# Attention of the first stage: one mask product for a chain of four heads, three probability buffers, value products four steps behind

## The chip, the core and the metric

The kernel runs on one core of a Trainium2 chip. The metric is the device time of one execution in microseconds (us); a version's time is the median of its runs. Engines are named as in the profile: PE (TensorE, matrix products; PEld its weight loads), DVE (VectorE), ACT (ScalarE), POOL (GpSimd) and SP (SyncE, which only issues DMAs here).

## What is computed

Two layers, each a cross-attention and a feed-forward part, all with residuals. The change is in the first cross-attention: 8 batches of 256 queries and 256 keys, 32 query heads of width 16 that share 8 groups of keys and values.

```
x = x + jnp.tanh(g_xattn[0]) * _L0_xattn_ref(_layernorm(x, axis=-1), ctx_2048, mask_SxS2_bc0, mask_BxS2_bk0, ...)
...
H, G = 32, 8; HD = 16; HPG = 4
q = X @ Wq.T + bq;  k = enc @ Wk.T + bk;  v = enc @ Wv.T + bv
scores = jnp.einsum('bgrqd,bgkd->bgrqk', q, k) / jnp.sqrt(HD)
scores = jnp.where(causal_mask, -jnp.inf, scores);  scores = jnp.where(padding_mask, -jnp.inf, scores)
w = jax.nn.softmax(scores, axis=-1)
out = jnp.einsum('bgrqk,bgkd->bgrqd', w, v) ... @ Wo.T + bo
```

## The kernel before

Everything is written as f16 high and low halves, so a product is three products (`three`, L140 to L142). The first attention is `phase_a`. Each engine has its own program (`on_sp`, `on_pe`, `on_act`, `on_pool`, `on_dve`), and semaphores order them; no scheduler moves anything. After a prologue each engine runs 8 bodies, one for each batch b, of NS = 32 steps n. Here T(n) means the moment at which PE begins step n of a body.

What a step does, in the order in which each engine is programmed:

- PE: the transposed scores of batch b (`turned_scores`, L748 and L750), keys on the partitions, for two query heads and one half kc of the keys, into one of two PSUM banks; then the products with the values of the step LAG = 3 back (`times_v`, L767, L769, L771, twelve small ones); then plain scores of batch b+1 (`scores`, L727 and L730), which serve only to find each query's maximum. On top of this, at fixed steps: output projection of batch b-1 (`turn_output`, then `output`, one slice of three 512-column products per step, OTURN and OUT), query projections of batch b+2 (PQ), key and value projections (PK), key transposes (L713), the transposes of the maxima (`turn_maxima`, L738, at NEG0 and NEG1).
- ACT: two exponentials of the bank, one to f16 (`ph`, L1031) and one to f32 (`prob`, L1032); at fixed steps the copies `high_q` (L934), `high_kv` (L945 to L951), `take_maxima` (L957), `high_output` (L961), `normal` (L970), and sums or signs of feed-forward weights for the next stage (`absolute`, L987, in bodies 0 to 3 at SUM_AT; `sign`, L996, in bodies 4 to 7 at CUT_AT and LAST_AT).
- POOL: `pl` = `prob` - `ph` (L1143), and at the steps of FRONT the halves of the next context and x tiles.
- DVE: the maxima (`maxima`, L1232), `low_q` (L1206), `low_kv` (L1214 to L1218), `normalise` (L1248, L1251) and others.
- SP: loads of weight pieces (L543) and contexts, DMA transposes of contexts and x (`place_ctx`, `place_x`), of the queries (`place_q`, L559), of the signed weights (`place_piece`, L577), and the copies of the negated maxima into the queries (`place_maxima`, L549). SP works through its list in program order; each entry waits for its own data.

The mask is added by a product of its own: `ident16` times `madd`, 512 columns. A chain is a row of products that add up in one bank. The first product of a chain adds the mask and the scores of one head; the next subtracts these scores and adds those of the next head (keys are stored as a pair, negated beside plain, and a 128-row query chunk holds two neighbouring heads). Before, a chain has two heads, so every second step of each bank has a mask product.

The waits that matter: exponential n waits for `turned_scores(n)` and for `pl` of step n-2 (two `prob` buffers); `turned_scores(n)` waits for the exponential of n-2; `times_v(n-3)` waits for `pl` of n-3. The query projection uses bank BM, which the turned maxima and the output of half 0 use too.

## Time and profile before

| | |
|---|---|
| time, median of 3 runs | 1663.49 us (1662.81 to 1663.49) |
| the profiled execution's own time | 1660.81 us |
| its span, first to last instruction | 1659.1 us |
| granted TensorE clock over the span | 0.984 of full speed |
| first exponential of the attention to the last | 78.7 to 490.6 us |

The span is cut by stage; the eight bodies are 412 us of it, 51.5 us each. A stretch's row gives each engine's busy time within it. In a row of the timeline the columns are start, duration, engine, line, operation, tiles and shape, count, and in brackets the engine's idle time before it with what ended it.

### The profile page before, as it was taken

What the parts mean: (1) busy time and instruction counts of PE and PEld (TensorE: products, weight loads), DVE (VectorE), ACT (ScalarE), POOL (GpSimd) and SP (SyncE); (2) the same over time, 40 slices, a digit from 0 to 9 for tenths busy, and PEclk for the clock granted to TensorE, in tenths of its full rate; (3) what the DMA queues carried; (4) which work ended last, traced back from release to release, by engine and by line L of the source; (5) the groups of instructions that cost most, each with busy time, mean ns of one, the idle gap of its engine ahead of it and who ended that gap; (6) DMA issues with size and microseconds to landing.
All of it is one profiled execution on the core that took longest, in us unless ns stands there. A gap on an engine that the chain in (4) does not pass through costs nothing. (4 is left out here: it accounts for less than half of the span.)

```text
span 1659.1 us, 29208 instructions
## 1 busy us (share of the span) xinstructions
PE 1576.7 (95%) x10826; PEld 828.4 (50%) x10826; DVE 944.3 (57%) x1947; ACT 710.2 (43%) x1311; POOL 831.6 (50%) x893
## 2 busy tenths in 40 slices
PE   5889999999779999999999989999999999999998
PEld 3456665666434444446565644444444444444443
DVE  5756766778847888735656442468454333322246
ACT  3288888888886666523323221211111111233321
POOL 3488887877884555533534244434342542022244
PEclk9899999999899999999999999999999999999999
DMA  7754645333254665433553427546453745388855
GB/s 189 169 119 100 119 94 110 89 80 75 73 130 95 127 121 102 96 83 77 109 124 80 96 65 159 119 97 158 90 108 92 153 111 115 77 190 195 188 154 189
DMA packets 453955, 195.67 MB, mean 118 GB/s; under 512 B 395500, under 2 KB 418286, under 8 KB 453816
## 3 DMA queue, kind: packets, MB, share of 16 engines
q1 hardware_dynamic: 440216, 171.26, 47.6%
q0 software_dynamic: 5680, 18.62, 4.4%
q10 hardware_dynamic: 7920, 3.93, 1.0%
q8 instruction: 88, 1.44, 0.4%
q14 instruction: 51, 0.42, 0.1%
HBM read 77.17 MB, written 22.81 MB: 60 GB/s over the span
## 5 line engine op out<-in xcount | busy, mean ns | idle before, releaser
L1143 POOL TENSOR_TENSOR a_pl<-a_prob,a_ph 128x512 f16<-128x512 f32 x256 | 296.0, 1170 | 74.6 <-ACT a_prob L1032 74.2
L1232 DVE TENSOR_REDUCE a_mx<-bank 128x2 f32<-128x512 f32 x256 | 173.2, 686 | 87.2 <-PE bank L730 85.7
L140 PE MATMUL bank<-XTh,d_whs 128*128 128x512 f16 x512 | 194.9, 381 | 3.9 <-PEq L89 2.4
L141 PE MATMUL bank<-XTl,d_whs 128*128 128x512 f16 x512 | 194.7, 380 | 0.0
L142 PE MATMUL bank<-XTh,d_wls 128*128 128x512 f16 x512 | 194.6, 380 | 0.0
L1031 ACT ACTIVATE a_ph<-bank 128x512 f16<-128x512 f32 x256 | 153.8, 601 | 59.2 <-PE bank L750 36.2
L2420 POOL CAST d_cut<-d_raw 128x512 f16<-128x512 f32 x90 | 57.1, 635 | 227.4 <-DMA d_raw<-in_L_ffn_sw 145.6
L1032 ACT ACTIVATE a_prob<-bank 128x512 f32<-128x512 f32 x256 | 154.0, 602 | 0.0
L2340 DVE TENSOR_TENSOR d_hid<-d_hid,bank 128x512 f32<-128x512 f32 x64 | 43.9, 686 | 169.2 <-PE bank L142 165.3
L2331 ACT ACTIVATE d_hid<-bank 128x512 f32<-128x512 f32 x64 | 38.2, 597 | 204.9 <-PE bank L142 204.9
L2335 ACT ACTIVATE d_hh<-d_hid 128x512 f16<-128x512 f32 x64 | 40.3, 630 | 194.2 <-DVE d_hid L2340 194.2
L2432 POOL DMA_INDIRECT e_x<-rows,d_who x39 | 37.1, 952 | 145.8 <-DMA e_xTl<-e_x 139.8
L2422 POOL TENSOR_TENSOR d_cut<-d_raw,d_cut 128x512 f16<-128x512 f32 x90 | 106.3, 1181 | 7.2
L767 PE MATMUL bank<-a_v,a_ph 128*128 128x17 f16 x1024 | 103.2, 172 | 5.3 <-POOL a_pl L1143 5.1
L730 PE MATMUL bank<-a_qk 128*128 128x256 f16 x512 | 100.1, 279 | 7.8 <-DVE a_mx L1232 7.6
L750 PE MATMUL bank<-a_qk 128*128 128x512 f16 x256 | 99.6, 389 | 6.8 <-ACT a_prob L1032 6.7
L2350 DVE SCALAR_TENSOR_TENSOR X<-bank,tg,X 128x512 f32<-128x512 f32 x112 | 76.3, 744 | 50.1 <-PE bank L142 50.1
L767 PEld LDWEIGHTS bank<-a_v,a_ph 128*128 128x128 f16 x1024 | 88.4, 97 | 28.7 <-POOL a_pl L1143 7.7
L771 PE MATMUL bank<-a_v,a_pl 128*128 128x17 f16 x1024 | 102.1, 171 | 0.0
L769 PE MATMUL bank<-a_v,a_ph 128*128 128x16 f16 x1024 | 101.9, 170 | 0.0
L1535 PE MATMUL bank<-b_wpj,b_hTh 128*128 128x512 f16 x256 | 97.0, 379 | 1.6 <-DMA b_hTl<-b_hcut 1.6
L140 PE MATMUL bank<-d_whd,d_hh 128*128 128x512 f16 x256 | 97.0, 379 | 1.5 <-DVE d_hl L2344 1.5
(350 smaller groups left out, 3978.1 us busy)
## 6 DMA issues: line engine op xcount, KB each, us to landing
d_raw<-in_L_ffn_w SPq DMA_DIRECT2D x48, 256.0 KB, 3.0
d_raw<-in_L_ffn_sw SPq DMA_DIRECT2D x42, 256.0 KB, 3.0
made<-e_y SPq DMA_DIRECT2D x39, 256.0 KB
a_stage<-in_L_ffn_w_fc SPq DMA_DIRECT2D x32, 256.0 KB, 2.9
a_stage<-in_L_ffn_w_proj SPq DMA_DIRECT2D x32, 256.0 KB, 3.0
a_fbuf<-in_ctx SPq DMA_DIRECT2D x16, 256.0 KB, 3.2
rows<-f_cut SPq DMA_DIRECT2D x16, 256.0 KB, 2.5
out_x<-X SPq DMA_DIRECT2D x16, 256.0 KB, 2.4
```

The costliest lines, as they stand in the source:

```text
L140: nc.tensor.matmul(out_ap, lhi, rhi, start=first, stop=False)
L141: nc.tensor.matmul(out_ap, lhi, rlo, start=False, stop=False)
L142: return nc.tensor.matmul(out_ap, llo, rhi, start=False, stop=last_one)
L730: last = nc.tensor.matmul(bk[:, r * S:(r + 1) * S], qT[:, par, 2 * g + r, tt * P:(tt + 1) * P], kT[:, par, 2 * g + half, :], start=False, ...
L767: nc.tensor.matmul(into[:, c:c + HD0 + 1], ph[:, n % NP, q], vv[:, b % 3, kc, g, 0:HD0 + 1], start=first, stop=False, skip_group_check=True)
L769: nc.tensor.matmul(into[:, c:c + HD0], ph[:, n % NP, q], vv[:, b % 3, kc, g, HD0 + 1:VW], start=False, stop=False, skip_group_check=True)
L771: last = nc.tensor.matmul(into[:, c:c + HD0 + 1], pl[:, n % NP, q], vv[:, b % 3, kc, g, 0:HD0 + 1], start=False, stop=(kc == 1), skip_grou ...
L1031: nc.scalar.activation(ph[:, n % NP, :], bank[BST + n % 2][:, :], ACT.Exp)
L1032: nc.scalar.activation(prob[:, n % 2, :], bank[BST + n % 2][:, :], ACT.Exp).then_inc(ev["E"], 1)
L1143: nc.gpsimd.tensor_tensor(pl[:, n % NP, :], prob[:, n % 2, :], ph[:, n % NP, :], ALU.subtract).then_inc(ev["L"], 1)
L1232: nc.vector.tensor_reduce(mx[:, h, tt, half, 2 * (g % 4):2 * (g % 4) + 2], bank[BS + m % 2][:, :].rearrange("p (r k) -> p r k", r=2), AX_X ...
L2422: nc.gpsimd.tensor_tensor(cut[:, i % RING, 1, :], raw[:, i % RING, :], cut[:, i % RING, 0, :], ALU.subtract).then_inc(p_lo, 1)
```

## The change

Chains run over four heads: the mask product stands only where j, the place in a chain of four, is 0, so at steps 0, 1, 8, 9, 16, 17, 24, 25 (before: at 0, 1, 4, 5, 8, 9, ...). One turned product of 512 columns becomes two of 256, since the two heads' query chunks are no longer neighbours. The queries need chunks (q0,q1), (q1,q2), (q2,q3) instead of (q0,q1), (q2,q3), so 30 chunks instead of 16: `place_q` issues 16 DMA transposes per batch instead of 8, the first of its two calls in two parts; for the first batches PE turns the additional chunks (`turn_early`) and ACT takes them (`take_early`). `place_maxima` issues three DMAs instead of two. There are three `prob` buffers (NR) and five `ph` and `pl` (NP), and LAG is 4. The x tiles have one buffer instead of two. NEG0 goes from step 27 to 20, so the maxima are turned between the two query projections, in bank BM. SUM_AT, CUT_AT, OTURN, OUT, FRONT and the steps of `normal`, `place_ctx`, `place_x` and `load_ctx` move.

```diff
-    NP = 4
-    prob = sb("a_prob", [P, 2, D])
+    NP, NR = 5, 3
+    prob = sb("a_prob", [P, NR, D])
...
-    on = sb("a_on", [P, 2, 2, D])
+    on = sb("a_on", [P, 2, D])
...
-    LAG = 3
+    LAG = 4
...
-    NEG0, NEG1 = 27, 4
-    OTURN, OUT = (5, 6), (7, 11)
+    NEG0, NEG1 = 20, 4
+    OTURN, OUT = (6, 7), (8, 12)
...
-    SUM_AT = [1, 5, 9, 13, 17, 21, 25, 29]
-    CUT_AT = [1, 6, 11, 17, 23, 28]
-    WO_AT = [12, 14, 16, 18]
+    SUM_AT = [1, 3, 9, 11, 17, 23, 29, 30]
+    CUT_AT = [1, 3, 9, 17, 23, 29]
+    WO_AT = [9, 14]
...
     def which(m):
-        u = m % 16
-        return u // 8, 4 * (m // 16) + 2 * (u // 4 % 2) + u % 2, u // 2 % 2
+        return m % 2, m // 16, m // 2 % 8
+
+    def key_chunk(h, r, j):
+        first = j == 0 or j == 4
+        return 8 * h + 4 * r + 2 * (j // 4) + (0 if first else 1)
+
+    def query_chunk(h, r, j):
+        if j % 2:
+            return 16 * h + j - 1 + r
+        return 16 * h + j + r if j % 4 == 0 else 16 * h + 8 + j - 2 + r
...
-                if b + 2 < B and n == PQ[1] + KC + 1:
-                    place_q(b + 2, 0)
+                for tt in range(2):
+                    if b + 2 < B and n == PQ[tt] + KC + 1 + tt:
+                        place_q(b + 2, 0, [tt])
...
-                if f < B and n == 10:
-                    place_ctx(f)
+                if f < B and n in (8, 12):
+                    place_ctx(f, [n // 12])
...
-                if f < B and n == 22:
-                    place_x(f)
+                if 3 < f + 1 < B and n == NS - 6:
+                    load_ctx(f + 1)
+                if f < B and n == NS - 4:
+                    place_x(f)
...
-            if half == 0:
+            if n % 8 < 2:
                 nc.tensor.matmul(bk[:, :].rearrange("p (r k) -> p r k", r=2), ident16[:, :],
                                  maddT[:, kc, :].unsqueeze(1).broadcast_to([P, 2, S]), start=True, stop=True)
-            nc.tensor.matmul(bk[:, :], kT[:, par, 2 * g + half, kc * P:(kc + 1) * P],
-                             qT[:, par, 2 * g:2 * g + 2, :].rearrange("p r q -> p (r q)"),
-                             start=False, stop=True, skip_group_check=True).then_inc(ev["ST"], 1)
+            for r in range(2):
+                last = nc.tensor.matmul(bk[:, r * S:(r + 1) * S], kT[:, par, key_chunk(h, r, j), kc * P:(kc + 1) * P],
+                                        qT[:, par, query_chunk(h, r, j), :], start=False, stop=True,
+                                        skip_group_check=True)
+            last.then_inc(ev["ST"], 1)
...
-                if b + 3 < B and n == 4:
+                if b + 3 < B and n == 3:
                     moments(b + 3)
```

Three places in the order of the instructions. First PE at step 4 of body 2, from the last product with the values on (`a_madd` is the mask); before:

```order
L771 MATMUL bank<-a_v,a_pl 128x17
L727 MATMUL bank<-a_madd,ident 128x512
L730 MATMUL bank<-a_qk 128x256 x2
L738 MATMUL bank<-ident,a_nmx 16x128 x2
L748 MATMUL bank<-a_maddT,ident 128x512
L750 MATMUL bank<-a_qk 128x512
```

And in the changed kernel:

```order
L817 MATMUL bank<-a_v,a_pl 128x17
L773 MATMUL bank<-a_qk 128x256 x2
L781 MATMUL bank<-ident,a_nmx 16x128 x2
L794 MATMUL bank<-a_qk 128x256 x2
L813 MATMUL bank<-a_v,a_ph 128x17
```

Both mask products of the place are gone, and the turned product is a pair. Second, PE at step 20 of body 2, from its plain scores on; before:

```order
L727 MATMUL bank<-a_madd,ident 128x512
L730 MATMUL bank<-a_qk 128x256 x2
L140 MATMUL bank<-a_wkvh,a_cTh 128x256
L141 MATMUL bank<-a_wkvl,a_cTh 128x256
L142 MATMUL bank<-a_wkvh,a_cTl 128x256
```

And in the changed kernel:

```order
L773 MATMUL bank<-a_qk 128x256 x2
L781 MATMUL bank<-ident,a_nmx 16x128 x2
L140 MATMUL bank<-a_wkvh,a_cTh 128x256
L141 MATMUL bank<-a_wkvl,a_cTh 128x256
L142 MATMUL bank<-a_wkvh,a_cTl 128x256
```

The transposes of the maxima now stand ahead of the last slices of the key projection. Third, SP's list from the end of body 1 into body 2, before:

```order
L559 DMA_TRANSPOSE a_qk<-a_qs 128x4x128 x4
L549 DMA a_qk<-a_nT 1x8x256 x2
L543 DMA a_stage<-in_L_ffn_w_proj 128x512
L516 DMA a_fbuf<-in_ctx 128x512 x2
L559 DMA_TRANSPOSE a_qk<-a_qs 128x4x128 x4
L543 DMA a_stage<-in_L_ffn_w_proj 128x512
L549 DMA a_qk<-a_nT 1x8x256 x2
```

And in the changed kernel, from `place_x` at step 28 of body 1 on:

```order
L559 DMA_TRANSPOSE a_xTh<-a_fcut 128x4x128
L560 DMA_TRANSPOSE a_xTl<-a_fcut 128x4x128
L565 DMA a_stage<-in_L_ffn_w_proj 128x512 x2
L582 DMA_TRANSPOSE a_qk<-a_qs 128x4x128
L586 DMA_TRANSPOSE a_qk<-a_qs 128x3x128
L582 DMA_TRANSPOSE a_qk<-a_qs 128x4x128
L586 DMA_TRANSPOSE a_qk<-a_qs 128x3x128
L582 DMA_TRANSPOSE a_qk<-a_qs 128x4x128
L586 DMA_TRANSPOSE a_qk<-a_qs 128x3x128
L582 DMA_TRANSPOSE a_qk<-a_qs 128x4x128
L586 DMA_TRANSPOSE a_qk<-a_qs 128x3x128
L565 DMA a_stage<-in_L_ffn_w_proj 128x512 x2
```

The query transposes of step 0 are eight instead of four, and the x transposes stand close ahead of them instead of at step 22.

## Rows read from the trace of the kernel before

**Rows 1.** The page: busy time of PE over the span.

```profile
PE 1576.7 (95%) x10826; PEld 828.4 (50%) x10826; DVE 944.3 (57%) x1947; ACT 710.2 (43%) x1311; POOL 831.6 (50%) x893
```

**Rows 2.** Timeline of PE, body 2, steps 1 to 3.

```profile
183.13 0.38 PE L748 MATMUL bank<-a_maddT,ident 128*128 128x512 f16 x1
183.35 0.38 PE L750 MATMUL bank<-a_qk 128*128 128x512 f16 x1
...
185.28 0.38 PE L730 MATMUL bank<-a_qk 128*128 128x256 f16 x2
185.50 0.38 PE L750 MATMUL bank<-a_qk 128*128 128x512 f16 x1
```

**Rows 3.** Stretches: bodies 0, 2, 5, 6, 7; last columns granted clock, DMA share, GB/s.

```profile
78.70:131.00 52.30, 45.90 (x577) 27.42 (x576) 31.26 (x59) 43.07 (x93) 42.89 (x41) 0.98 0.54 114
...
183.00:235.10 52.10, 49.87 (x637) 31.82 (x636) 34.89 (x65) 44.18 (x96) 43.69 (x42) 1.00 0.55 103
...
340.70:391.40 50.70, 49.46 (x636) 31.72 (x634) 36.41 (x65) 42.10 (x84) 37.14 (x32) 1.00 0.29 69
391.40:442.10 50.70, 43.20 (x566) 26.52 (x563) 43.23 (x84) 41.40 (x79) 42.63 (x40) 0.93 0.29 72
442.10:492.20 50.10, 40.25 (x510) 22.11 (x510) 28.54 (x54) 45.78 (x86) 43.98 (x41) 0.92 0.48 110
```

**Rows 4.** Timeline of PE: T(29) of body 1; then body 2's steps 6, 8, 28, 29.

```profile
178.36 0.38 PE L748 MATMUL bank<-a_maddT,ident 128*128 128x512 f16 x1
...
191.49 0.39 PE L730 MATMUL bank<-a_qk 128*128 128x256 f16 x2 [0.81 <-DVE a_mx L1232]
...
193.54 0.38 PE L748 MATMUL bank<-a_maddT,ident 128*128 128x512 f16 x1
...
227.54 0.39 PE L748 MATMUL bank<-a_maddT,ident 128*128 128x512 f16 x1
...
230.01 0.61 PE L713 MATMUL bank<-ident,a_ks 128*128 128x128 f16 x8 [1.13 <-DVE a_v L1218]
...
230.46 0.38 PE L748 MATMUL bank<-a_maddT,ident 128*128 128x512 f16 x1
```

**Rows 5.** Timeline of ACT, body 2, steps 1, 2 and 4.

```profile
184.62 0.59 ACT L1032 ACTIVATE a_prob<-bank 128x512 f32<-128x512 f32 x1
185.09 0.63 ACT L987 ACTIVATE a_tern<-a_stage 128x512 f16<-128x512 f32 x1
...
185.71 0.60 ACT L1031 ACTIVATE a_ph<-bank 128x512 f16<-128x512 f32 x1
...
188.14 0.60 ACT L1031 ACTIVATE a_ph<-bank 128x512 f16<-128x512 f32 x1 [0.38 <-POOL a_pl L1143]
```

**Rows 6.** Timeline of POOL, body 2, steps 3 and 4.

```profile
188.54 2.28 POOL L1143 TENSOR_TENSOR a_pl<-a_prob,a_ph 128x512 f16<-128x512 f32 x2
190.78 1.16 POOL L1080 TENSOR_TENSOR a_fcut<-a_fbuf,a_fcut 128x512 f16<-128x512 f32 x1
```

**Rows 7.** Timeline of all engines, body 2, step 20.

```profile
214.96 0.38 PE L730 MATMUL bank<-a_qk 128*128 128x256 f16 x2
215.07 0.69 DVE L1206 SCALAR_TENSOR_TENSOR a_qs<-bank,a_qs 128x512 f16<-128x512 f32 x1 [0.82 <-ACT a_qs L934]
```

**Rows 8.** SP's issues: body 0; bodies 2 to 3 (first the timeline, then the DMA view).

```profile
79.62 6.24 SPq L559 DMA_TRANSPOSE a_qk<-a_qs  x4
...
225.75 5.12 SPq L559 DMA_TRANSPOSE a_qk<-a_qs  x4
230.91 1.36 SPq L549 DMA_DIRECT2D a_qk<-a_nT  x2
...
a_qk<-a_qs SPq DMA_TRANSPOSE x52, 2.7
```

**Rows 9.** Weight loads in front of the paired products, whole attention.

```profile
L730 PEld LDWEIGHTS bank<-a_qk 128*128 128x128 f16 x512 | 41.5, 98 | 28.7 <-DVE a_mx L1232 10.6 <-issue 3.3
```

**Rows 10.** Stretch: body 0, from POOL's step 0 to its step 15.

```profile
79.83:105.34 25.51, 21.43 (x274) 12.14 (x273) 15.83 (x30) 20.79 (x42) 21.50 (x21) 0.97 0.44 100
```

More of the change, by code:

```diff
@@ L666, in q_of @@
                 pass
+            elif tt and b >= 2:
+                wait("nc", b - 1, 1, 2)
             elif tt:
@@ L716, in scores @@
         def scores(b, par, m):
-            tt, g, half = which(m)
-            bk = bank[BS + m % 2]
+            tt, h, j = which(m)
+            bk = bank[BS + tt]
             wait("M", b, m + 1, NS)
@@ L741, in turned_scores @@
         def turned_scores(b, par, n):
[L742 to L743 removed]
+            kc, h, j = which(n)
+            bk = bank[BST + kc]
             wait("E", b, n + 1, NS)
             if n % 16 == 0:
[L746 to L747 removed]
+                pe.wait_ge(ev[f"ng{h}"], 48 * (b + 1))
+            if n % 8 < 2:
                 nc.tensor.matmul(bk[:, :].rearrange("p (r k) -> p r k", r=2), ident16[:, :],
@@ L754, in times_v @@
+            last.then_inc(ev["ST"], 1)
         def times_v(b, n):
-            g, half, kc = n // 4, n // 2 % 2, n % 2
+            p, j, kc = n // 8, n // 2 % 4, n % 2
             if n % 8 == 0:
-                wait("ON", b, g // 2 + 1, G0 // 2)
-            wait("L", b, n + 3, NS)
-            into = bank[BAV + g // 2 % 2]
+                wait("ON", b, p + 1, G0 // 2)
+            wait("L", b, n + NR + 1, NS)
+            into = bank[BAV + p % 2]
             for r in range(2):
+                g = p + 4 * r
@@ L1017, in on_act @@
         high_kv(0, 1)
+        for i in range(2):
+            for tt in range(2):
+                take_early(0, 1, tt, i)
         for tt in range(2):
@@ L1021, in on_act @@
         take_maxima(0, 0)
+        for i in range(2):
+            for tt in range(2):
+                take_early(1, 0, tt, i)
         normal(2, 0)
```

250 lines of the change are left out of this document (143 added, 107 removed).

## Prediction

> **What bounds the kernel now.** I began with the page. PE is busy for 95% of the span [rows 1], but that is the union of overlapping products and says little here: a 512-column product is shown as 0.38 us, and the next starts 0.22 us after it; a pair of 256 columns takes 0.22 us together [rows 2]. The Trainium skill says the same of that column (Trainium Kernel Development and Optimization, Performance Expectations: matmul busy time is a bad metric because matmuls are pipelined). So I worked in distances between starts.
>
> Next the stretches of the bodies [rows 3]. Bodies 1 to 5 have PE busy for nearly all of their 52 us, with ACT and POOL at 44 and 43.5. Bodies 0, 6 and 7 leave PE idle for 6 to 10 us and are still 50 to 52 us long, so there the engines wait for each other in turn.
>
> Then the timeline of one steady body. From T(29) of body 1 to T(29) of body 2 it is 230.46 - 178.36 = 52.10 us, and falls into three parts [rows 4]: T(29) to T(8), 15.18 us; T(8) to T(28), 34.00 us; T(28) to T(29), 2.92 us. The middle part has a projection slice in every step up to 26, and PE runs without a wait worth naming: products bound it. The third part is a round trip: the key projection's last slice, ACT's copies, DVE's halves, and PE waits 1.13 us to turn the keys [rows 4]. In the first part PE has little to do. There ACT needs 0.47 us per exponential from start to start and 0.62 us for an `absolute` [rows 5], and POOL 1.12 us for a `pl` (188.54 to 190.78 for two) or a low half [rows 6]. With two `prob` buffers ACT may be only two steps ahead of POOL; it waits 0.38 us at step 4 [rows 5]. PE waits 0.81 us for the maxima at step 6 [rows 4], which are late because the moments of step 4 stand ahead of them on DVE.
>
> **The change, part by part,** for a steady body (1 to 3).
>
> Mask products in the middle part. Steps 12, 13, 20 and 21 lose two each: 8 x 0.215 = 1.72 us off a part that products bound. An output slice comes in from step 7 (now 8 to 15): 3 x 0.215 = 0.65. 34.00 - 1.72 + 0.65 = 32.93 us.
>
> The split of the turned product. Two of 256 columns start within the same 0.22 us as one of 512 [rows 2], so it costs nothing while the additional weight load is hidden. The loads of the plain scores, which have this very form, take 98 ns beside the products [rows 9]. The bound above is 256 x 0.098 = 25 us in all if none were hidden; I take 0, since rows 2 show the pairs as they run. The skill has a rule against this (TensorE: Matmul & The Clock Gate, Back-to-back issue gap): in a real stream the spacing is set by both the load and the product, and small products suffer. By that rule part of the 25 us would have to be paid; the trace does not agree for 256 columns, at 0.11 us each.
>
> The third part stays at 2.92: same steps, same copies. Only the 0.36 us copy of the maxima leaves ACT ahead of it; I count nothing.
>
> The first part. The moments stand one step earlier and `normalise` one later, so PE's 0.81 us should go. The third `prob` buffer lets ACT lead POOL by a step more (1.1 us), which covers POOL's additional jobs at steps 4 to 6. ACT then sets T(8): ten pairs of exponentials, 9.5, four `absolute` (29, 30, 1, 3), 2.5, the maxima's copy 0.3, and the 0.6 from T(29) to the first exponential: 12.9 us. That is the lower bound; the upper one is 15.18 as now. I take 13.4, near the lower bound, because the two named waits are what separates them.
>
> Against it, step 20. The maxima are now turned there into bank BM, and this must wait for `low_q` of the first half, which reads that bank. On the trace the plain scores of step 20 end at 214.96 + 0.22, and without the two masks 0.43 earlier, 214.75; `low_q` ends at 215.07 + 0.69 = 215.76 [rows 7]. PE waits 1.0 us, with key and query slices queued behind it, in the part that products bound. The wait is absent before, since the next writer of BM stood in step 21. It could be zero if PE came a step later; I keep 1.0.
>
> Sum: 32.93 + 2.92 + 13.4 + 1.0 = 50.25, 1.85 us less; for three bodies -5.5 us.
>
> SP's list. A transpose takes 1.28 us of SP's time (5.12 for four), 1.56 in body 0, and lands 2.7 us after its issue; two copies of maxima take 1.36 [rows 8]. A body's list grows by 8 transposes and 2 copies, 11.6 us, to about 42 of 50 us. It still fits, but from step 27 on it holds 4 + 4 + 8 transposes and two loads, 21.5 us. They start 4.7 us ahead of T(29) (225.75 against 230.46, rows 8 and 4), so end 16.8 after it. In bodies 1 to 3 what follows is a load needed at step 11, about 0.5 us late, hidden by PE's lead. In bodies 4 and 5 it is `place_piece` of step 1, landed at T(29) + 19.5, for which the `sign` of step 9 waits. ACT would be there at 13.4 + 1.8 + 0.6 + 0.95 = 16.8. So ACT waits 2.7 us; two score banks hide about 1.2 us of that, PE loses 1.5. Body 4: -1.85 + 1.5 = -0.35. Body 5 has no POOL jobs beside `pl` and less to win in the first part (-0.5): -1.72 + 0.65 - 0.5 + 1.0 + 1.5 = +0.9.
>
> Body 0. POOL's first fifteen steps take 25.51 us with 21.50 busy [rows 10]. They are not bound by products, so the third buffer and FRONT's new steps pay: I take 22.0, so -3.5 (bounds 0 and -4.0). The rest of that body: masks off, step 20's wait on, about even.
>
> Bodies 6 and 7. PE is not the bound; POOL is busy 42.6 and 44.0, ACT 41.4 and 45.8 of 50.7 and 50.1 [rows 3]. The buffer smooths, the new CUT_AT avoids the step of `high_output` in DVE and ACT. I take -1.5 and -1.0 (bounds 0 and -4 each).
>
> Prologue. 28 more transposes on PE and eight copies by ACT, a wait for all four query copies; half of the plain scores' masks gone; ACT is mostly idle there. Nothing, within 2 us either way.
>
> Total: -3.5 - 5.5 - 0.35 + 0.9 - 1.5 - 1.0 = -11 us. The later stages are unchanged and take the gain over. The sum is made on the profiled execution, 1660.8 us with 1.7 us outside the span; that is 2.7 below the median, and I carry the difference: 1663.5 - 11 = 1652.5 us.
>
> **The rivals.**
>
> Nearly all mask time comes back (0.14). 128 mask products go, 27.6 us; if step 20's wait and SP's delay stay hidden and ACT sets the first part at its lower bound: 52.1 - 49.0 for bodies 1 to 5, 15 us, with 4 + 3 + 3 elsewhere, 1639. PE's full busy time in bodies 1 to 5 speaks for it; POOL at 43.5 and ACT at 44 of then 49 us speak against it.
>
> The gain is absorbed (0.24). The work only moves to waits: ACT's four `absolute` in the unbound part, the wait at step 20, SP's list. With the first part at 14.8 instead of 13.4 and body 0 at half, -11 + 5 x 1.4 + 1.8: about 1661, from 1656 up.
>
> Slower, by SP's queue (0.08). At body 0's 1.56 us per transpose throughout, 24 transposes are 37.4 us and the rest 10 to 12: the list fills a body, and contexts, weights and x tiles come late in every one. It decides from about 1.5 us per transpose. At 3.5 us lost per body in six bodies, -11 + 21: 1673. The rows of bodies 2 and 3 at 1.28 speak against it.
>
> Slower, by weight loads that aren't hidden (0.02): -11 + 25, 1677.
>
> Slower or even, by the clock (0.03). The granted clock is 0.93 and 0.92 in bodies 6 and 7 [rows 3], where PE has idle time, against 1.00 in bodies 1 to 5. With fewer products PE has more idle time everywhere. Bodies 1 to 5 at 0.92 instead of 1.00 would cost their product-bound parts 8% of 35 us each, 14 us: 1666.
>
> **How the numbers follow.** Forecast 0.49, around 1652.5, from 1645 to 1659 by its bounds. The range 1641 to 1664 leaves out about 0.06 below and 0.13 above. A measurement of this kernel tells no change from 0.2%, 3.3 us. Faster than 1660.2: the forecast, the first rival and a good half of the absorbed case, 0.78. Slower than 1666.8: the queue, the loads, half of the clock, and a tail of the absorbed case, 0.11. Between, 0.11.
>
> **What would show it.** T(8) to T(28) of body 2 near 33.9 us with the wait, and PE's turned maxima at step 20 with about 1.0 us idle, released by DVE's `a_qs`. ACT without waits on POOL in steps 29 to 8. The `sign` of step 9 in bodies 4 and 5 with a wait for a DMA of `a_tern`. SP's sets of four transposes at 5.1 us. Body 0 shortened most. Wrong would be: clock below 1.00 in bodies 1 to 5, body 0 unchanged, or PE starts of the paired products more than 0.11 us apart.

## The result, and the profile after

The changed kernel takes 1670.34 us, median of 7 runs (1667.98 to 1675.61); the kernel before took 1663.49 in the 7 runs beside it. The ratio is 1.0045, with a 95% interval of 1.0028 to 1.0061: 7.5 us slower, where I had forecast 11 us faster. The time lies outside my range.

The stretches of the changed kernel, bodies 0, 2, 5, 6 and 7, answer to [rows 3]; the last row is a piece of body 2:

```profile
75.30:127.00 51.70, 44.08 (x575) 31.23 (x574) 33.64 (x61) 43.12 (x94) 42.48 (x40) 0.87 0.58 127
...
180.80:235.30 54.50, 48.82 (x652) 34.74 (x650) 35.75 (x69) 44.27 (x97) 43.64 (x41) 0.94 0.49 117
...
345.50:404.20 58.70, 50.04 (x655) 34.91 (x653) 37.94 (x68) 41.65 (x85) 37.76 (x33) 0.91 0.42 86
404.20:453.00 48.80, 41.55 (x590) 29.52 (x587) 44.02 (x89) 41.23 (x80) 41.74 (x40) 0.90 0.38 80
453.00:499.40 46.40, 38.43 (x529) 23.99 (x526) 28.33 (x58) 43.65 (x85) 43.15 (x40) 0.89 0.52 121
188.00:194.00 6.00, 4.68 (x43) 3.85 (x44) 3.82 (x8) 5.40 (x13) 4.66 (x6) 0.50 0.45 97
```

Bodies 6 and 7 are 2 us shorter each, as the change wants. Bodies 1 to 5 are longer, body 5 by 8 us, and the granted clock, 1.00 in them before, is 0.91 to 0.97. In the piece of 6 us it is 0.50, which is TensorE at 1.2 GHz. The eight bodies together take 424.1 us, 12.2 more than before; the stretch before them is 3.4 us shorter in this profile and the later stages 1.8 us, which leaves the 7.0 us between the spans of 1659.1 and 1666.1.

Where body 2 is longer shows on PE's timeline, at the places of [rows 4]: T(29) of body 1, steps 5 to 8, step 20, T(28), T(29).

```profile
176.24 0.38 PE L794 MATMUL bank<-a_qk 128*128 128x256 f16 x2
...
187.46 0.39 PE L773 MATMUL bank<-a_qk 128*128 128x256 f16 x2 [1.21 <-DVE a_mx L1298]
189.32 0.61 PE L794 MATMUL bank<-a_qk 128*128 128x256 f16 x2 [1.47 <-ACT a_prob L1099]
...
193.35 0.63 PE L791 MATMUL bank<-a_maddT,ident 128*128 128x512 f16 x1
...
216.01 0.28 PE L781 MATMUL bank<-ident,a_nmx 128*16 128x128 f16 x2 [0.90 <-DVE a_qs L1272]
...
227.89 0.38 PE L794 MATMUL bank<-a_qk 128*128 128x256 f16 x2
...
230.78 0.38 PE L794 MATMUL bank<-a_qk 128*128 128x256 f16 x2
```

T(29) to T(8) is 193.35 - 176.24 = 17.11 us, against 15.18 before and 13.4 forecast. T(8) to T(28) is 34.54, T(28) to T(29) 2.89. In this body the loss sits in the first part. PE waits there first for DVE's maxima, then for ACT; after the second wait its products are half as fast (0.63 instead of 0.38 us in the records). ACT's timeline says what it stood for at its step 3:

```profile
187.57 0.63 ACT L1048 ACTIVATE a_tern<-a_stage 128x512 f16<-128x512 f32 x1 [2.16 <-DMA a_stage<-in_L_ffn_w_proj]
...
365.69 0.72 ACT L1057 ACTIVATE a_tern<-a_stage,a_unround 128x512 f16<-128x512 f32 x1 [6.47 <-DMA b_wfc<-a_tern]
```

The last row is step 9 of body 5, in the middle part of that body. SP's timeline, which answers to [rows 8], has both causes: the load of step 29 (the first of the two at 183.81) stands behind query and x transposes, and in body 5 the piece of step 1 (363.24) stands at the end of a row of transposes that begins at 337.42.

```profile
172.46 1.50 SPq L582 DMA_TRANSPOSE a_qk<-a_qs  x1
...
181.85 1.91 SPq L560 DMA_TRANSPOSE a_xTl<-a_fcut  x1
183.81 1.05 SPq L565 DMA_DIRECT2D a_stage<-in_L_ffn_w_proj  x2
...
337.42 1.20 SPq L582 DMA_TRANSPOSE a_qk<-a_qs  x1
...
351.06 1.19 SPq L582 DMA_TRANSPOSE a_qk<-a_qs  x1
...
360.50 2.70 SPq L586 DMA_TRANSPOSE a_qk<-a_qs  x1
363.24 1.26 SPq L604 DMA_TRANSPOSE b_wfc<-a_tern  x1
```

### The profile page after: what moved, and what is told of

The parts are those of the page before. It is cut to its first block and busy times, and to the rows that moved or that the text cites. A ratio compares the mean times of both kernels' runs of the same rounds, so it can differ in the third digit from the quotient of the medians.

```text
span 1666.1 us, 29689 instructions
## 1 busy us (share of the span) xinstructions
PE 1560.3 (94%) x11014; PEld 849.8 (51%) x11014; DVE 948.8 (57%) x1979; ACT 716.3 (43%) x1319; POOL 832.1 (50%) x893
## 3 DMA queue, kind: packets, MB, share of 16 engines
q1 hardware_dynamic: 463128, 176.74, 47.9%
## 5 line engine op out<-in xcount | busy, mean ns | idle before, releaser
L794 PE MATMUL bank<-a_qk 128*128 128x256 f16 x512 | 106.7, 293 | 23.3 <-ACT a_prob L1099 23.0
L773 PE MATMUL bank<-a_qk 128*128 128x256 f16 x512 | 102.3, 284 | 15.8 <-DVE a_mx L1298 15.6
L142 PE MATMUL bank<-d_whd,d_hl 128*128 128x512 f16 x256 | 97.0, 379 | 0.0
```

Source lines behind the costliest of these rows:

```text
L142: return nc.tensor.matmul(out_ap, llo, rhi, start=False, stop=last_one)
L773: last = nc.tensor.matmul(bk[:, r * S:(r + 1) * S], qT[:, par, query_chunk(h, r, j), tt * P:(tt + 1) * P], kT[:, par, key_chunk(h, r, j), ...
L794: last = nc.tensor.matmul(bk[:, r * S:(r + 1) * S], kT[:, par, key_chunk(h, r, j), kc * P:(kc + 1) * P], qT[:, par, query_chunk(h, r, j), ...
```

## The experiments

Sixteen variants were measured, each beside the kernel before. The table gives their ratios, and the length of each body in the profiled execution, from ACT's first exponential of one body to that of the next (body 7: to the start of its last one). The bodies come from one execution each. The code behind the attention is the same in all of them but for a few semaphores, and the stretch from the last exponential to the end still differs by up to 7.7 us between the profiles (1164.8 to 1172.5), so a difference of a few us between two medians need not come from the bodies.

| kernel | median us | ratio, interval | bodies 0 to 7, us |
|---|---|---|---|
| before | 1663.5 | | 52.4, 52.0, 52.1, 53.2, 52.3, 50.8, 50.7, 48.5 |
| changed | 1670.34 | 1.0045 (1.0028, 1.0061) | 51.7, 53.8, 54.5, 56.1, 54.1, 58.7, 48.8, 46.4 |
| a1_lists | 1660.31 | 0.9971 (0.9955, 0.9986) | 51.1, 51.8, 51.8, 53.5, 53.0, 54.5, 47.9, 46.4 |
| a2_q14 | 1668.51 | 1.0020 (1.0006, 1.0035) | 50.7, 54.3, 54.2, 55.4, 54.2, 56.4, 49.0, 46.3 |
| a3_fill | 1680.54 | 1.0092 (1.0075, 1.0109) | 51.3, 54.6, 54.6, 55.6, 56.1, 59.2, 50.3, 46.8 |
| a4_rings | 1677.36 | 1.0066 (1.0047, 1.0084) | 52.2, 54.5, 55.9, 55.3, 54.1, 57.8, 51.4, 47.9 |
| b1_moments | 1666.85 | 1.0038 (1.0021, 1.0056) | 52.1, 52.9, 53.9, 54.6, 53.5, 57.6, 47.9, 46.3 |
| b2_lists_moments | 1655.48 | 0.9954 (0.9937, 0.9970) | 51.5, 50.2, 52.6, 56.1, 52.1, 51.5, 46.9, 46.2 |
| b3_all | 1655.39 | 0.9947 (0.9931, 0.9964) | 49.0, 54.4, 51.4, 51.7, 53.0, 50.4, 48.0, 46.3 |
| b4_fill | 1669.75 | 1.0035 (1.0021, 1.0048) | 50.3, 53.7, 53.7, 54.7, 54.4, 53.6, 50.6, 47.0 |
| a6_oldsum | 1667.62 | 1.0022 (1.0008, 1.0036) | 49.6, 53.8, 53.0, 53.7, 55.6, 55.7, 50.1, 46.2 |
| c1_front | 1673.45 | 1.0053 (1.0037, 1.0069) | 56.2, 54.6, 53.2, 56.8, 58.7, 51.7, 47.0, 46.4 |
| c2_front_oldsum | 1671.99 | 1.0054 (1.0036, 1.0072) | 56.3, 55.5, 53.6, 55.2, 59.0, 50.2, 49.3, 46.2 |
| c3_front_q14 | 1665.79 | 1.0014 (0.9995, 1.0034) | 54.8, 53.4, 52.3, 55.6, 53.6, 50.3, 48.0, 46.3 |
| e1_lists2 | 1661.17 | 0.9982 (0.9965, 1.0000) | 50.8, 51.8, 51.8, 54.3, 54.4, 52.6, 48.0, 46.4 |
| e2_extras | 1698.97 | 1.0210 (1.0190, 1.0230) | 59.2, 60.8, 60.5, 58.9, 58.4, 52.8, 51.8, 47.7 |
| e3_spread | 1665.77 | 1.0011 (0.9997, 1.0025) | 51.9, 51.6, 51.7, 52.7, 53.0, 51.8, 52.0, 48.5 |
| e4_list | 1707.73 | 1.0245 (1.0217, 1.0272) | 53.3, 58.4, 63.3, 57.6, 67.4, 58.1, 51.6, 48.5 |

### SP's list relieved

```diff
-                if b + 1 < B and n == 0:
+                if b + 1 < B and n == 2:
                     place_q(b + 1, 1)
...
-                if f < B and n == NS - 4:
+                if f < B and n == NS - 2:
                     place_x(f)
```

> The changed kernel, with two entries of SP's list moved and nothing else: the eight query transposes of step 0 stand at step 2, behind the loads and placements of step 1, and the x transposes of step 28 stand at step 30, behind the load of step 29. List theory (my first): the stage loads and the placements are late because SP stands in transposes; ACT waits for them (2.2 to 2.6 us at step 3 of bodies 1 to 3, 7.0 us at step 9 of body 5), PE runs dry behind ACT and the clock falls after it. Then these waits are gone, bodies 1, 2, 3 are about 2 us shorter each, body 5 about 6, and with the clock that is held up the time is 1655 to 1660 us. Step-20 theory (the loss is the wait for the low half at step 20, before the maxima are turned): SP's list is slack, the time stays at 1667 to 1671. Clock theory (fewer products alone let the granted clock fall): the half-clock time in the bodies stays near 68 us and the time within 3 us of the changed kernel's.

Measured: 1660.31 us, 10 below the changed kernel and at the upper edge of what the list theory gave, from two moved places in a list. No `absolute` waits for a load any more, bodies 1 to 3 are 2.0 to 2.7 us shorter, body 5 by 4.2, and bodies 1 and 2 are again at clock 1.00. The list theory holds; the step-20 theory and the clock theory, as sole causes, fall. PE's timeline of body 2 shows what was hidden behind it, two waits for DVE's maxima (1.21 and 0.99 us), and T(8) at 188.31; T(29) of body 1 was at 173.36, so the first part is 14.95 us, and T(8) to T(28) is 222.28 - 188.31 = 33.97.

```profile
173.36 0.38 PE L794 MATMUL bank<-a_qk 128*128 128x256 f16 x2
...
184.58 0.39 PE L773 MATMUL bank<-a_qk 128*128 128x256 f16 x2 [1.21 <-DVE a_mx L1298]
186.47 0.39 PE L773 MATMUL bank<-a_qk 128*128 128x256 f16 x2 [0.99 <-DVE a_mx L1298]
...
188.31 0.38 PE L791 MATMUL bank<-a_maddT,ident 128*128 128x512 f16 x1
...
222.28 0.38 PE L794 MATMUL bank<-a_qk 128*128 128x256 f16 x2
```

DVE's timeline of the same kernel has the reason: moments, their two short operations, a maximum, a copy of keys and the normalisation in one row, busy from 180.68 to 187.6.

```profile
180.68 0.68 DVE L1298 TENSOR_REDUCE a_mx<-bank 128x2 f32<-128x512 f32 x1
181.27 1.28 DVE L1243 BATCH_NORM_STATS2 a_stats<-X 128x6 f32<-128x512 f32 x2
...
182.87 1.06 DVE L1249 TENSOR_SCALAR a_ve<-a_mv 128x2 f32<-128x2 f32 x1
183.84 0.68 DVE L1298 TENSOR_REDUCE a_mx<-bank 128x2 f32<-128x512 f32 x1
184.45 0.68 DVE L1291 COPY a_qk<-bank 128x1024 f16<-128x1024 f16 x1
...
185.73 1.88 DVE L1298 TENSOR_REDUCE a_mx<-bank 128x2 f32<-128x512 f32 x3
```

### The wait at step 20 taken away

```diff
-    PQ, PK = (15, 21), (19, 25)
+    PQ, PK = (14, 21), (19, 25)
```

> The changed kernel, with the first query projection one step earlier (its slices at steps 14 to 17, its halves at 18), so that the low half is done well before the maxima are turned at step 20. Step-20 theory: PE's wait of 1.0 to 1.3 us in six bodies goes, 6 to 8 us off, 1661 to 1664 us. List theory: the wait at step 20 goes as well, but the bodies are longer in their first third, and what PE gains from step 20 on it has partly given to the round trip of steps 28 and 29: 2 to 5 us off. Clock theory: PE has even more slack elsewhere, no change.

Measured: PE's waits before the turned maxima fall from 12.5 us (12 waits) to 3.6 in the whole program, T(8) to T(28) of body 2 is 34.03 instead of 34.54, and the median is 2 us lower (4 us by the ratios, whose intervals overlap a little). The wait exists as I had forecast it, 0.9 us, but of the 0.7 us that go in body 2 the body keeps 0.1, since its first part is longer by as much as the middle part gained. The wait was a term of my sum, so it doesn't explain why the sum failed.

### The removed products put back

```diff
+            if n % 8 in (4, 5):
+                nc.tensor.matmul(bk[0:P // 2, :].rearrange("p (r k) -> p r k", r=2), zero[:, :],
+                                 maddT[:, kc, :].unsqueeze(1).broadcast_to([P, 2, S]), start=False, stop=True,
+                                 skip_group_check=True)
```

and the same for the plain scores.

> The changed kernel, with a product of 512 columns by zeros (added into 64 rows of the same bank) in each place where the kernel before had its second mask, so that PE has the work of before and everything else is of after. Clock theory: the half-clock time in the bodies falls from 68 us towards the 16 us of before, and the time is the same or shorter, 1662 to 1670 us, in spite of 128 more products. List theory: the waits for a_stage and a_tern stay as they are; the part of bodies 1 to 5 that products bound is 1.7 us longer each, and the time is 1675 to 1682 us; the clock recovers only where the idle stretches get shorter than now.

Measured: 1680.54, 10 us above the changed kernel, as the list theory had it. But bodies 1 to 5 together are only 2.9 us longer (280.1 against 277.2), although each has 16 more products, and bodies 1 to 4 ran at clock 1.00. Body 2, then its T(29) of body 1 and T(8), and ACT's wait for the load of step 3:

```profile
182.40:237.10 54.70, 53.36 (x668) 35.23 (x666) 36.32 (x69) 44.34 (x98) 43.73 (x41) 1.00 0.53 115
```

```profile
177.56 0.40 PE L799 MATMUL bank<-a_maddT,a_zero 128*64 128x512 f16 x1
...
192.85 0.38 PE L796 MATMUL bank<-a_maddT,ident 128*128 128x512 f16 x1
...
188.45 0.63 ACT L1057 ACTIVATE a_tern<-a_stage 128x512 f16<-128x512 f32 x1 [1.36 <-DMA a_stage<-in_L_ffn_w_proj]
```

ACT still waits for the load, and yet the first part is 192.85 - 177.56 = 15.29 us, 1.8 less than the 17.11 of the changed kernel and 0.3 more than the 14.95 of a1_lists. So most of what the late load costs in the first part is paid at half clock, and the wait itself is the smaller share: PE's waits there add up to 3.2 us in the changed kernel and 2.7 in a1_lists. (The products put back also fill PE's waits, to 0.3 us in all, so a3_fill alone doesn't part the two.) The same shows in steps 6 to 8, T(6) to T(9), which took 6.42 us at half rate in body 2 of the changed kernel and 4.18 at full rate in body 2 of b2_lists_moments, below. The clock theory holds in part, then: the clock fell where there were fewer products and a late load in one place. Fewer products and 2.7 us of waits, as in bodies 1 and 2 of a1_lists, did not bring it down.

### The buffers of before

```diff
-    NP, NR = 5, 3
+    NP, NR = 4, 2
...
-    LAG = 4
+    LAG = 3
```

> The changed kernel, with the buffers of before: two of prob, four of ph and pl, products three steps behind. If the deeper buffers give what I forecast for them (body 0 3.5 us, the first third of the bodies about 1 us each, bodies 6 and 7 1.0 to 1.5 us), the time is 8 to 12 us longer, 1678 to 1682. List theory: in bodies 1 to 3 ACT stands at the load anyway, so only bodies 0, 6 and 7 lose, 3 to 6 us, 1673 to 1676. If the deeper buffers are themselves the harm (products further behind, all in a bunch at a body's start), it is faster than 1668.

Measured: 1677.36, 7 us longer by the medians and 3.5 by the ratios, whose intervals overlap; the median lies between the ranges of the two theories. Bodies 1 to 5 are together as long as with the deeper buffers (277.6 against 277.2), bodies 0, 6 and 7 lose 0.5, 2.6 and 1.5. That is the pattern of the list theory, and it speaks for the deeper buffers in bodies 6 and 7, though it is one profile against one. POOL's steps 0 to 15 of body 0, on which my term for that body rests, take 22.5 us here with two `prob` buffers and 22.4 in the changed kernel with three (25.5 before): what shortened them was not the third buffer.

### DVE's moments, alone and with the list

```diff
-                if b + 3 < B and n == 3:
+                if b + 3 < B and n == 9:
                     moments(b + 3)
-                if b + 3 < B and n == 8:
+                if b + 3 < B and n == 12:
                     mean(b + 3)
...
-                    if n == 5:
+                    if n == 10:
                         deviation(b + 3)
```

> The changed kernel, with the moments of a body taken by DVE at step 9 instead of step 3 (POOL's power at 10 instead of 5, the mean at 12 instead of 8). DVE theory: the change stacked 2.7 us of moments, a copy of keys and a normalisation in steps 3 and 4, where PE's steps are shortest, so PE waits 1.2 us (2.2 us once SP's list is relieved) for the maxima. In the changed kernel alone ACT stands at the load of step 3 at the same time, so DVE's share is mostly hidden: 1 us or less a body in bodies 0 to 4, 1664 to 1670 us. If DVE was the cause by itself and the loads only waited beside it, the gain is 2 us a body, 1660 to 1662.

Measured: 1666.85. The five waits of `absolute` for loads are still there (8.6 us), and bodies 1 to 3 are 0.6 to 1.5 us shorter: mostly hidden behind the load, as expected.

For the next run the moments stand at step 9 too, SP's list is relieved as in a1_lists, and the eight query transposes are split:

```diff
-                if b + 1 < B and n == 0:
-                    place_q(b + 1, 1)
+                if b + 1 < B and n in (2, 6):
+                    place_q(b + 1, 1, [n // 6])
...
-                if f < B and n == NS - 4:
+                if f < B and n == NS - 2:
```

> The changed kernel with SP's list relieved (x transposes behind the load of step 29, four query transposes at step 2 and four at step 6) and the moments at step 9. Two causes in a row, SP's list and then DVE: with both gone PE's waits for the maxima (2.2 us in bodies 1 to 3, 1.6 in 0 and 4) and for the placed maxima in body 5 (1.8) go, bodies 1 and 2 come near the 50.25 us that I forecast, 8 to 10 us below the run with the lists alone: 1650 to 1653 us. If the moments only push DVE's lateness to step 10, in the part that products bound, the gain is under 3 us, 1657 to 1660.

Measured: 1655.48, 15 us below the changed kernel and 7.7 below the kernel before by the ratio. It is a version that beats both, but it lies between my two ranges. PE's timeline of body 1, T(29), T(8), T(28), T(29):

```profile
124.05 0.38 PE L794 MATMUL bank<-a_qk 128*128 128x256 f16 x2
...
137.22 0.38 PE L791 MATMUL bank<-a_maddT,ident 128*128 128x512 f16 x1
...
171.34 0.38 PE L794 MATMUL bank<-a_qk 128*128 128x256 f16 x2
...
174.22 0.38 PE L794 MATMUL bank<-a_qk 128*128 128x256 f16 x2
```

That is 13.17 + 34.12 + 2.88 = 50.17 us. Two single stalls remain in this profile: POOL stood 6.0 us for a written context in body 2 (my list puts the second half of the query transposes ahead of it, a likely reason that was not tried), and DVE's product of 2 elements took 4.43 us in body 3.

### The early projection on top

> The run with lists and moments mended, and the first query projection one step earlier. With the first third of a body free of waits the wait for the low half at step 20 is on the path: 0.7 us (what the early projection took off the stretch from step 14 to 20) to 1.2 us in six bodies, 4 to 7 us below the run without it, about 1646 us. If the slack is taken by turned outputs and the round trip again, as when it was tried alone (2 us), 1649 to 1651.

Measured: 1655.39, the same as without it. The wait at step 20 of body 1 fell from 0.9 to 0.2 us; in its place stands a wait of 2.4 us for POOL's `pl` there. My expectation of 4 to 7 us was wrong, and so was the smaller one beside it.

### The products put back, without the waits

> The run with lists and moments mended, with the 512-column products by zeros in the places of the removed masks. Mask products in the part that products bound are worth 1.72 us a body as I forecast, and little elsewhere: 1.7 x 6 plus up to 3, so 10 to 13 us longer than the run without them. In the changed kernel itself putting them back cost 10 us with the waits in place, 3.6 of it in bodies 1 to 5. Clock theory: they keep the granted clock up (under 15 us at half rate in the bodies, against some 30 without), and cost only 3 to 6 us.

Measured: 1669.75, 14 us longer, at clock 1.00 in bodies 0 to 5, so just beyond even my larger expectation of 10 to 13. Of the 15.3 us between the two profiled spans 10.4 lie up to the end of the attention, 4.9 in the unchanged stages behind it. In the stretches (body 0 and body 1, without and with the products) the clock shows too: body 0 runs at 0.89 without them and at 1.00 with them, and is no longer for it, in one profile of each.

```profile
77.10:128.60 51.50, 44.36 (x581) 30.67 (x579) 33.11 (x62) 42.96 (x94) 42.45 (x40) 0.89 0.60 123
128.60:178.70 50.10, 46.43 (x651) 33.15 (x649) 36.87 (x69) 43.55 (x97) 43.36 (x41) 1.00 0.54 125
```

```profile
76.70:126.90 50.20, 46.12 (x597) 30.73 (x595) 32.18 (x62) 42.59 (x93) 42.37 (x40) 1.00 0.59 132
126.90:180.70 53.80, 52.96 (x668) 35.25 (x666) 35.19 (x69) 44.31 (x98) 43.74 (x41) 1.00 0.49 115
```

The price of a product by zeros is higher than that of a mask, though. It has 64 columns of weights, and around it PE leaves gaps:

```profile
158.28 0.27 PE L142 MATMUL bank<-a_wkvh,a_cTl 128*128 128x256 f16 x1
158.48 0.40 PE L799 MATMUL bank<-a_maddT,a_zero 128*64 128x512 f16 x1
158.81 0.39 PE L803 MATMUL bank<-a_qk 128*128 128x256 f16 x2
```

The next product starts 0.33 us after it, a mask's 0.215 after; and it starts 0.20 after a product of 256 columns, 0.11 the usual distance. That is 0.42 us each, with eight in the middle part: 3.4 us. Its T(8) to T(28) is 36.45, 2.5 more than the 33.97 of a1_lists, and of the wait at step 20 some 0.9 us are gone in it: 3.4. So the middle part pays for every product in full, and my 8 x 0.215 = 1.72 for the masks in it stands, by this working; masks of the true size were not put back. What they are worth in all was not measured either: the 14 us are an upper bound.

### ACT's extras at the old steps

```diff
-    SUM_AT = [1, 3, 9, 11, 17, 23, 29, 30]
-    CUT_AT = [1, 3, 9, 17, 23, 29]
+    SUM_AT = [1, 5, 9, 13, 17, 21, 25, 29]
+    CUT_AT = [1, 6, 11, 17, 23, 28]
```

> The changed kernel, with ACT's extras at the steps of before (absolute values at 1, 5, ..., 29, signs at 1, 6, 11, 17, 23, 28). The load of step 29 is then wanted at step 9 and the piece placed at step 28 at step 6. If the loads were late because SP's longer list met the changed spread, the wait of 2.2 us at step 3 of bodies 1 to 3 goes with the spread alone, and DVE's wait (2.2 us) stays: 1 us a body, and in bodies 4 and 5 the sign waits elsewhere: 1664 to 1668 us. If SP's list is late for everything it holds, the wait only moves to another step and the time is 1669 to 1672.

Measured: 1667.62. No `absolute` waits for a load, DVE's wait of 2.0 us stays; in body 5 a sign waits 4.8 us for a placed piece. A load that has more steps until its use bears the late list. The time is in the range that I gave for this case, 1664 to 1668.

### The x tile's normalisation later

```diff
-                    if n == 10:
+                    if n == 13:
                         deviation(b + 3)
...
-                if b + 3 < B and n == 12:
+                if b + 3 < B and n == 14:
                     mean(b + 3)
...
-                 17: (x_high, 0), 19: (x_low, 0), 22: (x_high, 1), 24: (x_low, 1)}
+                 19: (x_high, 0), 21: (x_low, 0), 24: (x_high, 1), 26: (x_low, 1)}
```

with ACT's copies at 16 and 18, on top of b2_lists_moments.

> The changed kernel with SP's list and the moments mended as before, and the normalisation of the next x tile one to three steps later (power at 13, mean at 14, ACT's copies at 16 and 18, POOL's halves at 19, 21, 24, 26), so that POOL does not stand for the written context (6.0 us once) and DVE's 2-element product does not stand beside POOL's full row (4.4 us once). If those two stretches were what is left, bodies 2 and 3 come to 50.5 to 51.5 us and the time to 1648 to 1651. If they are single events of one profile, the median stays at 1653 to 1656.

> The run c1_front with ACT's extras at the steps of before. The changed spread puts four absolute values (2.5 us) between steps 29 and 3, where ACT sets the length of a body's first third; the old one puts two there. If ACT sets it, 1.2 us a body come off in bodies 1 to 3 and something in 4 and 5: 4 to 5 us below c1_front. If the round trip of the keys sets the start of that third, nothing.

> The run c1_front with the first query projection one step earlier. The wait at step 20 (1.2 us) goes for 0.5 to 0.7 us a body, as in the two runs that had it; if nothing takes it back, 3 to 4 us below c1_front. In those two runs the medians moved by 2 and 0 us; if that is the rule, less than 2 us.

Measured: 1673.45, 1671.99 and 1665.79, 18, 16 and 10 us above the version they were meant to better. Neither range of c1_front holds. Against it c2_front_oldsum is level by the ratios (1.0054 and 1.0053), so the second branch of its expectation holds, nothing from ACT's steps; c3_front_q14 is 7.7 us lower, more than either branch gave. The line of the mean on DVE in c1_front says why the three are slow:

```profile
L1253 DVE SCALAR_TENSOR_TENSOR a_nmean<-a_mv,a_rstd x8: 149/1657/3318, 11.5 to 325.9; 128x2 f32<-128x2 f32 x8
its engine sat idle before it (us, times) until:
  POOL a_rstd L1134: 17.9, 6
```

DVE reaches the mean one step after POOL's power, POOL is behind by more than that, and DVE waits 3 us each time with the maxima queued behind it (six waits of 17.9 us together, against six of 4.4 together in b2_lists_moments, with the mean two steps after). The mean itself takes longer too, 2.2 us in bodies 1 to 3 and 3.3 in body 0, against 1.1 as a rule. In addition PE waits 1.3 to 2.0 us in each of bodies 1 to 4 for query transposes; that they stand in SP's list behind the x transposes, whose halves now end at step 26, is the likely reason, and was not tried by itself. The late normalisation moved two stalls seen once and put a wait into every body.

### What of SP's list does the harm

> The changed kernel with the relieved list of b2_lists_moments (four query transposes at step 2, four at step 6) and the moments at step 3 as the change put them. The run with all eight at step 2 had 1660.3, the run with this list and the moments at step 9 had 1655.5. Between them lie 4.8 us: 3 us in body 5, where the maxima were behind eight transposes (the list's share), and 1.6 us in body 1 (the moments' share, less in others because single stalls came in). If both hold, 1657 to 1659 us. If the moments do nothing, 1655; if the split does nothing, 1660.

This is the changed kernel with the list of b2_lists_moments and the moments back at step 3. Measured: 1661.17, above the 1657 to 1659 that I expected. Against b2_lists_moments the moments are worth 5.7 us by the medians and 4.7 by the ratios; the split of the eight transposes gives nothing against a1_lists (1660.31). PE's wait for the maxima is 2.2 us in body 1 of e1_lists2, and there is none in body 1 of b2_lists_moments.

The next three are the kernel before with parts of the change. Four transposes more in each placement:

```diff
+                    if b < B - 1:
+                        i = count[0]
+                        count[0] += 1
+                        if i:
+                            sp.wait_ge(k_scr, 16 * i)
+                        sp.dma_start_transpose(scr[:, i % 2], wqh[:, u, :]).then_inc(k_scr, 16)
```

> The kernel before with four more transposes in each placement of query chunks (eight more a body, each of 128x512 from a constant tile into a scratch tile; nothing reads it), so that SP's list is as long as the changed one's. If a longer list is harmful by itself, as in my slower rival, +5 to +10 us. If it needs the changed spread to be felt, because before a load had eight steps from its issue to its use, within 2 us of the kernel before.

Measured: 1698.97, 35 us longer, far beyond my larger expectation. The added transposes also wait for each other's landing, which leaves gaps of 0.55 to 0.8 us in SP's row, so this list is somewhat longer than the changed one's. Not the loads were late (no `absolute` waits in it) but the maxima: the kernel before turns them at step 27, and SP issues their copies behind eight transposes of step 26. SP's and PE's timeline, body 3:

```profile
253.59 1.27 SPq L569 DMA_TRANSPOSE a_scr<-a_wqh  x1
254.90 1.36 SPq L551 DMA_DIRECT2D a_qk<-a_nT  x2
```

```profile
257.52 0.58 PE L756 MATMUL bank<-a_maddT,ident 128*128 128x512 f16 x1 [7.85 <-DMA a_qk<-a_nT]
```

PE's five waits for these copies are 32.8 us of the 35. So turning the maxima at step 20, where the change does it, is probably what makes its own list bearable, and the 0.9 us of wait there is cheap beside 7.85; the changed kernel with the maxima at step 27 was not tried.

The extras' places alone (the reverse of the edit of a6_oldsum, on the kernel before):

> The kernel before with ACT's extras at the changed steps (absolute values at 1, 3, 9, 11, 17, 23, 29, 30; signs at 1, 3, 9, 17, 23, 29). SP's list has four query transposes at step 26 and four at step 0. ACT gets 1.2 us more in the first third of bodies 1 to 3 and is short of room there because of two prob buffers: +1 us a body in 1 to 3, the rest even: 1665 to 1668 us. If the spread were harmless, 1662 to 1664.

Measured: 1665.77. That is in the range that I gave, but its ratio of 1.0011 (0.9997 to 1.0025) can't be told from 1, bodies 1 to 3 are at 51.6 to 52.7, no longer than before, and there is no wait for a load: nearly harmless alone.

Both, and the x transposes at step 28:

> The kernel before with both, and the x transposes at step 28 instead of 22: SP's list and ACT's spread of the changed kernel, with the mask products, buffers, banks and the turned maxima of before. If the two together are what took the gain, the load of step 29 comes late for step 3 here too (ACT waits about 2 us for a_stage in bodies 1 to 3, and for a placed piece at step 9 of body 5), and the time is 1672 to 1680 us, 8 to 16 above the kernel before. If the loss needed the changed kernel's fewer products, under 1668.

Measured: 1707.73, far above my 1672 to 1680. What I expected of the mechanism is there: ACT waits for the loads as in the changed kernel, 7.0 us in six waits (8.3 in five there), and 5.3 us in body 5 for a placed piece:

```profile
199.07 0.63 ACT L995 ACTIVATE a_tern<-a_stage 128x512 f16<-128x512 f32 x1 [2.07 <-DMA a_stage<-in_L_ffn_w_proj]
```

The wait for loads needs the longer list and the extras close behind it together (neither e2_extras nor e3_spread has one), and it comes without any change to products or banks. Whether it also needs the x transposes at step 28, which only this run has of the three, was not tried. The time itself doesn't carry over to the changed kernel: PE waits 13.7 us for the late maxima, which that kernel doesn't do, and 13.2 us for POOL's `pl`, and the rest of the 44 us is open.

## Why the prediction was wrong

The sum failed in two sentences, one on SP's list and one on DVE's moments. Against the forecast bodies 1 to 3 came out 12.6 us too long, body 5 7.0, body 0 2.8 and body 4 2.1, bodies 6 and 7 1.5 us shorter.

**SP's list (the step that failed).** I had the length of the list about right (transposes of 1.27 us, some of 1.5 to 2.7), and then looked at the wrong entry of it: "what follows is a load needed at step 11, about 0.5 us late, hidden by PE's lead". That is the load of step 1. The load of step 29 stands eight query transposes ahead of it, but behind four query and four x transposes, is needed at step 3, and was the one on the path: issued at 183.81, used at 187.57, 2.2 us late. The change had moved the extras from a spacing of four or more steps to 29, 30, 1, 3, and I had costed the move for ACT alone. In body 2 the list costs 2.2 us of the first part (17.11 against 14.95 with the two places moved), and in body 1 1.7. Of the 2.2 us 0.5 is more waiting of PE, the rest its products at half clock; in a3_fill, where the clock stays up, 0.3 is left in all. So the late load was the trigger and the half clock behind it the larger part of the price, and my sum had neither. "Hidden by PE's lead" had no row to it.

**The moments.** "The moments stand one step earlier and normalise one later, so PE's 0.81 us should go." It became 1.2 us in the changed kernel, and 2.2 in two waits once the load was in time (a1_lists). The moments (2.7 us with the small operations) moved into the steps in which PE is shortest, with the second copy of keys right behind and the normalisation after it. With both mended the first part is 13.17 us in body 1, and I had written 13.4. So the first part comes near the sum once nothing else stands before it; whether the third `prob` buffer allows it, as I had argued, was not tried with list and moments mended.

**The middle part and step 20.** Forecast 32.93 + 1.0 of wait = 33.93; 33.97 in a1_lists (34.54 in the changed kernel, whose step 8 ran at half clock). The split of the turned product costs nothing: pairs of 256 columns start 0.22 us apart from what follows, as before. The third part is 2.89.

**Bodies 4 and 5.** I had named the sign of step 9 that waits for the piece of step 1, and sized it at 2.7 us of ACT and 1.5 of PE. It was 6.5 us of ACT in body 5, and PE waited 4.9 us behind it. SP issued that piece at 363.24, 22.0 us after T(29) at 341.20 and not 16.8: the row before it began 3.8 us ahead of T(29), at 337.42, not 4.7, and took 25.8 us, not 21.5, with the placed piece of step 29 in it, which I had left out, and two transposes of 2.4 and 2.7 us. In body 4 no sign waits for a piece in this profile. Bodies 4 and 5 are 1.8 and 7.9 us longer than before where I had -0.35 and +0.9.

**Bodies 0, 6 and 7.** -0.7, -1.9 and -2.1 against -3.5, -1.5 and -1.0. In body 0 the place that I had named did shorten: POOL's steps 0 to 15 took 22.4 us, forecast 22.0. But not by the third buffer (22.5 without it), and the rest of the body gave 2.4 us back, with PE waiting 2.0 us behind a late load of ACT's. Body 0 is at clock 0.87, and in b4_fill 16 products more leave it no longer, which suggests that the masks' time came back as clock there. The stretch before body 0 is 3.4 us shorter in this profile. It ends at 75.0 to 78.3 in the kernels of the table made from the changed one and at 78.1 to 79.6 in those made from the one before, so some 2 us may be a gain of the change, at the edge of my "within 2 us"; single profiles don't show more.

**The clock rival.** I gave it 0.03, as a loss by itself. It happened, at 0.91 to 0.97, and a clock under 1.00 in bodies 1 to 5 was one of my own signs of being wrong. But it came as a follower: products gone and a late load in the same place. Where load and moments were mended (b2_lists_moments) the clock in bodies 1, 4 and 5 was 1.00 with as few products; where the products were put back (a3_fill) it was 1.00 in bodies 1 to 4 in spite of the late loads. By the stretches bodies 1 to 5 hold about 34 us at half rate (twice 1 minus the clock, times the length). The Trainium skill (TensorE: Matmul & The Clock Gate, Terms) puts the penalty at about the throttled time times 1 minus K/N (K/N is the granted share of the clock), which makes an estimate of 17 us here. The runs don't confirm so much: for body 2 alone it gives 3.3 us (54.5 x 0.06), and the place read directly, steps 6 to 8, gave 2.2. A part of the time at half rate is time in which PE waits anyway.

**The total.** With list and moments mended the change gives -7.7 us (interval -10.5 to -5.0), against a forecast of -11. So the mechanism was right, its size somewhat too large, and it was undone by the orders on two other engines' lists. How much of the -7.7 belongs to the chain of four is not shown: the moments at step 9 were never tried on the kernel before, where PE waits 0.81 us a body for the same maxima. The absorbed rival and the rival by SP's queue had the right place between them; the queue rival's condition (1.5 us per transpose throughout) was wrong, since it decides at 1.27 as soon as one short-dated load stands behind it.

## What to carry to other kernels

When an in-order issuing list grows, take each entry behind the growth and count from its issue to the step in which its data is used; the one with the shortest date decides, and moving the users' steps changes the dates as much as moving the entries. When work moves to another step of a second engine, add up that engine's whole step against the shortest steps of the engine that waits for it, not against the average. A term that saves the bound engine time pays only while nothing else makes that engine wait in the same stretch: here a few places in two lists were worth 15 us, and 128 removed products 14 at most. And such a wait can cost more than its own length: here most of the price was the half clock after it.

## What the runs showed of the hardware

DVE's product of 2 elements a partition (two tiles of the state buffer as inputs) takes 0.15 us where POOL is idle, 1.1 us as a rule in the bodies of b2_lists_moments, and once 4.43 us. In that case POOL had a full row of work, and the product ended when POOL paused. The three runs with the later normalisation have it at 2.2 us beside two POOL instructions and at 3.3 beside three. The case of 4.43 us, DVE, then POOL:

```profile
248.61 4.43 DVE L1253 SCALAR_TENSOR_TENSOR a_nmean<-a_mv,a_rstd 128x2 f32<-128x2 f32 x1 [0.31 <-POOL a_rstd L1134]
```

```profile
248.53 1.17 POOL L1209 TENSOR_TENSOR a_pl<-a_prob,a_ph 128x512 f16<-128x512 f32 x1
249.64 1.18 POOL L1147 TENSOR_TENSOR a_fcut<-a_fbuf,a_fcut 128x512 f16<-128x512 f32 x1
250.75 2.28 POOL L1209 TENSOR_TENSOR a_pl<-a_prob,a_ph 128x512 f16<-128x512 f32 x2
```

The Trainium skill (SBUF — State Buffer, Who interferes with whom) says that a DVE instruction with two inputs there contends with a GpSimd instruction that reads it, and that the order of issue decides who blocks. The kind agrees, and by these starts POOL's first instruction (248.53) did come before DVE's product (248.61). But the product stood through the three POOL instructions behind it too, which the order of issue alone does not give.

A product with 64 columns of weights among products with 128 costs 0.33 us to the next start instead of 0.215, and starts 0.09 later itself. And DMA transposes of the same form take SP 1.27 us mostly, and 1.5 to 2.7 in 21 of the 170 that it issues between the starts of bodies 0 and 7 of the changed kernel; the runs don't say why.
